# Last stage of a graph network: the own messages gathered plainly into buffers of their own and added by VectorE

## The chip, the cores and the metric

One core of one Trainium2 chip runs the whole network in a single launch. The metric is the device time of that launch in microseconds. The engines are TensorE (PE in the rows, with its weight loads as PEld), VectorE (DVE), ScalarE (ACT), GpSimd (POOL) and SyncE (SP, which here only issues DMAs).

## The reference, cut to what matters

The network has four layers over 10000 nodes (padded to 10240) of 512 features: graph attention, a mixture of 16 experts, a graph convolution of two steps, and a mixture of 8 experts. The change lies in the last kernel stage, which ends the convolution and does the second mixture:

```python
self_term = diag[:, None] * (x @ W0)
msgs = edge_vals[:, None] * (x @ W1)[edge_src]
neigh = segment_sum(msgs, edge_dst, num_segments=n)
h = relu(self_term + neigh + b)          # second step of the convolution
y = (h + x) * 0.5
...
logits = xf @ router_w                    # xf: layer-normed rows
for e in range(E):
    h = relu(xf @ w1[e] + b1[e]) @ w2[e] + b2[e]
    out = out + w[:, e] * layernorm(xf + h, gamma[e], beta[e])
```

`self_term + b` is in HBM as `own` when the stage begins, and the summed messages of a node that has any are a row of `message2`; a node without messages points to a row of zeros.

## The kernel before

`dense1_phase` works on 20 groups of 512 nodes (`NG`, `GR`), each group as 4 tiles `t` of 128 nodes (`T`, `P`) with 512 features in the free dimension. It is a pipeline written out by hand: every engine has a `body(i, c_)`, which `bodies` runs for c_ = 0, then in a loop of 4 passes with 4 bodies each, then four more times, 21 in all. In body g an engine works for several groups at once: the end of group g-1, the experts of group g, the transposes of g+1, the sums of g+2 and the loads of g+3. Within an engine the order is the order of the code; between engines there are counting semaphores.

The way of a tile of group g before the experts:

- SyncE loads the own rows into `own[n]`, n = g % 2 (`load_own`, L2299), once `summed` says that the buffer is free.
- GpSimd copies the row numbers to `at`, waits for `own_in`, and gathers from `message2` with an indirect DMA that adds to what lies in `own[n]` (`gather`, L2342); it raises `msg_in`.
- ScalarE waits for `msg_in` and does 0.5 * relu in place with a sum over features (`half`, L2379). That comes last in its body. The next body begins with two `norm` (L2408) for the transposes.
- ScalarE scales the loaded `y` (`scale_y`), VectorE adds (`sum_`, L2540), ScalarE squares, VectorE and GpSimd (`power`) make mean and scale, ScalarE does `norm`, TensorE transposes the tile (`turn`, L2744), ScalarE copies the high part (`high`, L2413) and VectorE makes the rest (`low`, L2564).

VectorE's body begins with `coefficients` of group g-1 (L2628 on), then `mean_of` (L2533, needs the four `half` of g+2), `routing` (L2596 on), the first `low`, and ends with `finish` of g-1, whose last instruction is L2661 for tile 3 and waits for TensorE's last product of the body. TensorE's body begins with `up(g, 0)`, twelve matmuls; then `turn(g+1, 0)`, `up(g, 1)`, `turn_coef`, `turn(g+1, 1)`, the cross products, `turn` 2 and 3, logits, squares (L2762), and the products of g-1. `turn` t needs the `norm` of its tile and the `low` of the tile before.

Of the kernel before, what the change touches and what calls it, by code (L numbers as in the profile page):

```python
# [24 lines left out]
ALU = mybir.AluOpType  # L25
# [3 lines left out]
P = 128  # L29
D = 512  # L30
# [3 lines left out]
T = 4  # L34
# [6 lines left out]
EP = ET * P  # L41
# [6 lines left out]
XS = 4  # L48
# [2166 lines left out]
def dense1_phase(nc, a, k, ex, out):  # L2215
# [5 lines left out]
    with ExitStack() as stack:  # L2221
        c = Core(nc, stack, "d1")
        x3 = [c.sb(f"x3{n}", [P, T, D]) for n in range(XS)]
        xf, res = c.sb("xf", [P, T, D]), c.sb("res", [P, T, D])
        own = [c.sb(f"own{n}", [P, T, D]) for n in range(2)]
        squared = c.sb("squared", [P, T, D], BF16)
        at = c.sb("at", [P, T], I32)
        gain = c.sb("gain", [P, T])
        xh, xl = ([c.sb(f"{n}{i}", [P, KC, GR], F32R) for i in range(2)] for n in ("xh", "xl"))
# [27 lines left out]
        y_in = [[c.sem(f"y_in{u}{t}") for t in range(T)] for u in range(XS)]  # L2257
        own_in = [[c.sem(f"own_in{n}{t}") for t in range(T)] for n in range(2)]
        msg_in, out_done = ([c.sem(f"{n}{t}") for t in range(T)] for n in ("msg_in", "out_done"))
        at_made, relu_done, gains, affine, summed = (c.sem(n) for n in ("at_made", "relu_done", "gains", "affine", "summed"))  # L2260
        means, squares_made, stats, pow_done, shifted, normed = (
            c.sem(n) for n in ("means", "squares_made", "stats", "pow_done", "shifted", "normed"))
# [22 lines left out]
        def in_range(i, c_, ahead):  # L2285

            return not isinstance(i, int) or 0 <= c_ + ahead < NG
# [41 lines left out]
        @block.gpsimd  # L2329
        def _(pool):  # L2330
            def gather(i, c_):
                g, n = i * XS + c_, c_ % 2
                if later(i, c_):
                    for t in range(T):
                        pool.wait_ge(msg_in[t], 16 * g)
                hold(pool)
                pool.tensor_copy(at[:], k.slot["d"][:, ds(T * g, T)]).then_inc(at_made, 1)
                pool.wait_ge(at_made, g + 1)
                for t in range(T):
                    pool.wait_ge(own_in[n][t], i * 32 + 16 * (c_ // 2 + 1))  # L2340
                    hold(pool)
                    pool.indirect_dma_start(own[n][:, t, :], None, k.message2[:, :],  # L2342
                                            bass.IndirectOffsetOnAxis(ap=at[:, t:t + 1], axis=0),
                                            bounds_check=EP + P - 1, compute_op=ALU.add).then_inc(msg_in[t], 16)

            def power(g):
                pool.wait_ge(stats, g + 1)
                pool.tensor_tensor(rs[:], ve[:], k.half_neg[:, 0:T], ALU.pow).then_inc(pow_done, 1)

            def power2(g):  # L2350
                pool.wait_ge(vars_, NVAR * g + NVAR)
                pool.tensor_tensor(rs2[:].rearrange("p t n -> p (t n)"), var2[:].rearrange("p t n -> p (t n)"),
                                   k.half_neg[:, 0:T * 2], ALU.pow).then_inc(pow2_done, 1)

            def body(i, c_):
                g = i * XS + c_
                if in_range(i, c_, 3):
                    gather(i, c_ + 3)
                if in_range(i, c_, 2):
                    power(g + 2)  # L2360
                if in_range(i, c_, 0):
                    power2(g)

            gather(0, 0)
            gather(0, 1)
            power(0)
            gather(0, 2)
            power(1)
            bodies(pool, body)

        @block.scalar
        def _(act_):
            def half(i, c_, t):

                g, n = i * XS + c_, c_ % 2
                act_.wait_ge(msg_in[t], 16 * g + 16)
                if t == 0 and later(i, c_):
                    act_.wait_ge(means, g)
                act_.activation(own[n][:, t, :], own[n][:, t, :], ACT.Relu, scale=0.5,  # L2379
                                accum_out=own_sum[:, t:t + 1]).then_inc(relu_done, 1)  # L2380
# [127 lines left out]
        def _(v):  # L2508
# [7 lines left out]

            def wide(t_):
                return t_.unsqueeze(2).broadcast_to(S3)

            def gains_of(i, c_):  # L2520
                g = i * XS + c_
                if later(i, c_):
                    v.wait_ge(affine, 4 * g)
                hold(v)
                v.tensor_scalar(gain[:], k.dev[:, ds(T * g, T)], 0.5, None, ALU.add).then_inc(gains, 1)

            def mean_of(i, c_):
                g = i * XS + c_
                v.wait_ge(relu_done, 4 * g + 4)
                if later(i, c_):  # L2530
                    v.wait_ge(squares_made, 4 * g)
                    v.wait_ge(shifted, NSHIFT * g)
                v.tensor_scalar(less_mean[:], own_sum[:], -1.0 / D, None, ALU.mult).then_inc(means, 1)  # L2533
# [15 lines left out]
            def shifts(i, c_):  # L2549

                g, u = i * XS + c_, c_ % XS
                s = Steps(v, shifted, NSHIFT * g)
                v.wait_ge(pow_done, g + 1)
                s(v.tensor_copy(pair[u][:, :, 0], rs[:]))
                s(v.tensor_tensor(pair[u][:, :, 1], less_mean[:], rs[:], ALU.mult))
                s.link(v.tensor_tensor(spread_sq[:], square_sum[:], rs[:], ALU.mult))
                s.link(v.scalar_tensor_tensor(msq[:], spread_sq[:], 1.0 / D, rs[:], ALU.mult, ALU.mult))
                s(v.tensor_tensor(base[c_ % 2][:, :, EXPERTS1:LOGITS], wide(msq[:]),
                                  ex.square[:].unsqueeze(1).broadcast_to(S3), ALU.add))
                assert s.n == NSHIFT  # L2560
# [91 lines left out]
            def finish(i, c_, t):  # L2652

                g, u = i * XS + c_, c_ % XS
                v.wait_ge(x_done, 4 * g + t + 1)
                if later(i, c_):
                    v.wait_ge(out_done[t], 16 * g)
                v.tensor_tensor(res[:, t, :], x3[u][:, t, :], pox[t][:], ALU.mult).then_inc(mul_done, 1)
                v.wait_ge(one_done, 4 * g + t + 1)
                v.wait_ge(mul_done, 8 * g + 2 * t + 1 + 16)  # L2660
                v.tensor_tensor(res[:, t, :], res[:, t, :], po1[t][:], ALU.add).then_inc(mul_done, 1)  # L2661

            def body(i, c_):
                g, n, n1 = i * XS + c_, c_ % 2, (c_ + 1) % 2
                front, mid, main, behind = (in_range(i, c_, ahead) for ahead in (2, 1, 0, -1))
                if behind:
                    coefficients(g - 1, n1, (c_ - 1) % XS)
                if front:
                    mean_of(i, c_ + 2)
                if main:  # L2670
                    routing(g, n)
                if mid:
                    low(g + 1, n1, 0)
                if main:
                    hidden_low(g, n, 0)
                if front:
                    sum_(i, c_ + 2, 0)
                if main:
                    hidden_low(g, n, 1)
                if mid:  # L2680
                    low(g + 1, n1, 1)
                if front:
                    sum_(i, c_ + 2, 1)
                if behind:
                    scale(g - 1, n1, 0)
                if mid:
                    low(g + 1, n1, 2)
                if main:
                    quadratic(g, n, 0)
                if behind:  # L2690
                    weighted_low(g - 1, 0)
                if front:
                    sum_(i, c_ + 2, 2)
                    sum_(i, c_ + 2, 3)
                if mid:
                    low(g + 1, n1, 3)
                if behind:
                    scale(g - 1, n1, 1)
                if main:
                    quadratic(g, n, 1)  # L2700
                if behind:
                    weighted_low(g - 1, 1)
                if front:
                    variance_of(i, c_ + 2)
                    if in_range(i, c_, 3):
                        gains_of(i, c_ + 3)
                    shifts(i, c_ + 2)
                if behind:
                    finish(i, c_ - 1, 0)
                if main:  # L2710
                    variance(g, n)
                if mid:
                    logits_of(g + 1, n1)
                if behind:
                    for t in range(1, T):
                        finish(i, c_ - 1, t)

            gains_of(0, 0)
            mean_of(0, 0)
            for t in range(T):  # L2720
# [1 line left out]
            variance_of(0, 0)  # L2722
            gains_of(0, 1)
            shifts(0, 0)
            mean_of(0, 1)
            for t in range(T):
                sum_(0, 1, t)
# [2 lines left out]
            gains_of(0, 2)  # L2730
            shifts(0, 1)
            logits_of(0, 0)
            bodies(v, body)

        @block.tensor
# [229 lines left out]
```

## Time and profile before

| | |
|---|---|
| median of 3 runs | 2803.28 us (2800.49 to 2804.03) |
| the profiled execution | 2806.13 us, its span 2803.8 us |
| mean granted TensorE clock | 0.932 of full speed |
| TensorE, VectorE, ScalarE, GpSimd busy over the span | 87%, 63%, 41%, 24% |
| last stage | from about 2166 us to the end |

The page cuts the span into 40 slices of 70 us; the last nine are the last stage. The busy share is an average over an engine's order of work: an engine that idles may still be the one that is waited for at one point of each body, and an engine that waits long may be waiting where nobody needs it. So the shares are read together with the chain that ended last and the timeline of a single turn from body to body.

### The profile page before, as it was taken

To read this page: it belongs to the slowest core of one execution; us is meant where nothing else is said; L and a number is where in the kernel's file an instruction comes from. 1 tells how busy PE (TensorE), PEld (TensorE's weight loads), DVE (VectorE), ACT (ScalarE), POOL (GpSimd) and SP (SyncE) were. 2 spreads that over 40 slices of the span, in tenths; PEclk is the share of its full clock that TensorE was granted. 3 is DMA by queue.
4 is the path that set the end of the run, shared out by engine and by line. 5 is a ranking of instruction groups with operands and counts; after the bars stand their busy time and mean duration, and the time that the engine had idled before them with its cause. 6 is when DMAs were issued, how large, how long until landed. Compare 5 with 4: busy or idle time off the path is not lost. (4 is left out here: it accounts for less than half of the span.)

```text
span 2803.8 us, 37672 instructions
## 1 busy us (share of the span) xinstructions
PE 2428.5 (87%) x10876; PEld 1881.2 (67%) x10876; DVE 1772.8 (63%) x4089; ACT 1139.5 (41%) x2071; POOL 670.9 (24%) x675
## 2 busy tenths in 40 slices
PE   5698829399999999999957999999966499999998
PEld 4465617277777777777745888888854377777776
DVE  7454287577777777777544555555556377777775
ACT  6453301344354453444343222222232565665651
POOL 5444300311121111211021221221221333333320
PEclk8799959699999999999978999999987699999999
DMA  4112001411211212211043334334352655656531
GB/s 134 46 31 52 11 4 70 156 61 50 87 69 67 90 56 80 89 50 57 31 157 105 130 128 132 129 126 133 118 160 90 171 132 132 163 129 165 135 105 46
DMA packets 156248, 271.68 MB, mean 97 GB/s; under 512 B 35618, under 2 KB 36258, under 8 KB 155878
## 3 DMA queue, kind: packets, MB, share of 16 engines
q1 hardware_dynamic: 122854, 202.74, 21.5%
q0 software_dynamic: 33280, 67.71, 10.8%
q8 instruction: 36, 0.59, 0.1%
q14 instruction: 78, 0.64, 0.1%
HBM read 186.35 MB, written 100.41 MB: 102 GB/s over the span
## 5 line engine op out<-in xcount | busy, mean ns | idle before, releaser
L1053 POOL TENSOR_TENSOR d_rs<-d_ve,net_half_neg 128x4 f32<-128x4 f32 x60 | 61.2, 1019 | 563.0 <-DVE d_ve L1109 471.0
L1931 ACT ACTIVATE conv_h<-conv_h 128x512 f32<-128x512 f32 x80 | 50.6, 632 | 310.4 <-DVE conv_h L1893 310.4
L2342 POOL DMA_INDIRECT d_own<-message,d_at x80 | 130.6, 1633 | 162.6 <-DMA d_own<-own 142.6
L1863 DVE TENSOR_TENSOR conv_yl<-conv_pty,conv_yh 128x512 fp32r<-128x512 f32 x80 | 55.4, 692 | 180.1 <-ACT conv_yh L1927 168.0
L1374 ACT ACTIVATE d_act_out<-d_pa 128x512 f32<-128x512 f32 x80 | 46.7, 584 | 243.7 <-PE d_pa L67 243.7
L65 PE MATMUL d_po<-d_w_hi,d_hh 128*128 128x512 f32 x320 | 132.2, 413 | 14.0 <-DVE d_x L1200 14.0
L65 PE MATMUL conv_p<-conv_w_hi,conv_yh 128*128 128x512 f32 x320 | 133.8, 418 | 0.6 <-DVE conv_yl L1863 0.6
L65 PE MATMUL d_pa<-d_xh,d_w_hi 128*128 128x512 f32 x320 | 132.4, 414 | 0.5 <-DVE d_w_lo L1126 0.5
L1066 POOL DMA_INDIRECT d_val<-values,d_at x80 | 87.8, 1098 | 185.7 <-DVE d_x L1187 165.6
L65 PE MATMUL d_pc<-d_xh,d_w_hi 128*128 128x512 f32 x320 | 131.6, 411 | 0.0
L66 PE MATMUL d_pa<-d_xl,d_w_hi 128*128 128x512 f32 x320 | 128.9, 403 | 0.0
L67 PE MATMUL d_pa<-d_xh,d_w_lo 128*128 128x512 f32 x320 | 128.7, 402 | 0.0
L65 PE MATMUL conv_p<-conv_w_hi,conv_hh 128*128 128x512 f32 x320 | 126.2, 395 | 1.4 <-DVE conv_hl L1863 1.4
L66 PE MATMUL conv_p<-conv_w_lo,conv_yh 128*128 128x512 f32 x320 | 127.3, 398 | 0.0
L67 PE MATMUL conv_p<-conv_w_hi,conv_yl 128*128 128x512 f32 x320 | 127.1, 397 | 0.0
L67 PE MATMUL d_pc<-d_xh,d_w_lo 128*128 128x512 f32 x320 | 126.9, 397 | 0.0
L66 PE MATMUL d_pc<-d_xl,d_w_hi 128*128 128x512 f32 x320 | 126.6, 396 | 0.0
L67 PE MATMUL conv_p<-conv_w_hi,conv_hl 128*128 128x512 f32 x320 | 126.6, 396 | 0.0
L66 PE MATMUL conv_p<-conv_w_lo,conv_hh 128*128 128x512 f32 x320 | 126.5, 395 | 0.0
L67 PE MATMUL d_po<-d_w_hi,d_hl 128*128 128x512 f32 x320 | 126.3, 395 | 0.0
L66 PE MATMUL d_po<-d_w_lo,d_hh 128*128 128x512 f32 x320 | 126.1, 394 | 0.0
L1486 PE MATMUL d_ptr<-net_ident,d_xf 128*128 128x128 f32 x320 | 52.8, 290 | 61.8 <-ACT d_xf L1363 51.2
(513 smaller groups left out, 7213.3 us busy)
## 6 DMA issues: line engine op xcount, KB each, us to landing
d_x<-in_x SPq DMA_DIRECT2D x20, 1024.0 KB, 7.2
y<-d_y SPq DMA_DIRECT2D x80, 256.0 KB, 2.0
conv_yin<-y SPq DMA_DIRECT2D x80, 256.0 KB, 2.7
h<-conv_h SPq DMA_DIRECT2D x80, 256.0 KB, 2.0
own<-conv_own SPq DMA_DIRECT2D x80, 256.0 KB, 2.0
d_own<-own SPq DMA_DIRECT2D x80, 256.0 KB, 4.1
d_x<-y SPq DMA_DIRECT2D x80, 256.0 KB, 2.8
out<-d_res SPq DMA_DIRECT2D x80, 256.0 KB, 2.5
```

The source lines that it names most:

```text
L65: te.matmul(out, lhs[0], rhs[0], start=first, stop=False, skip_group_check=True)
L66: te.matmul(out, lhs[0], rhs[1], start=False, stop=False, skip_group_check=True)
L67: return te.matmul(out, lhs[1], rhs[0], start=False, stop=last, skip_group_check=True)
L1053: pool.tensor_tensor(rs[n][:], ve[n][:], k.half_neg[:, 0:T], ALU.pow).then_inc(pow_done[n], 1)
L1066: pool.indirect_dma_start(val[:, t, :], None, k.values[:, :], bass.IndirectOffsetOnAxis(ap=at[:, t:t + 1], axis=0), bounds_check=EP + P - ...
L1374: act_.activation(act_out[:, cc % 2, :], pa[cc % 2][:], ACT.Tanh, scale=0.5).then_inc(tanh_done, 1)
L1486: last = pe.transpose(ptr[:, kc * P:kc * P + P], xf[:, t, kc * P:kc * P + P], k.ident[:])
L1863: v.tensor_tensor(lo[:, t % 2, :], bank[t % 2][:], hi[:, t % 2, :].bitcast(F32), ALU.subtract)\
L1931: act_.activation(h[:, t, :], h[:, t, :], ACT.Relu).then_inc(h_made, 1)
L2342: pool.indirect_dma_start(own[n][:, t, :], None, k.message2[:, :], bass.IndirectOffsetOnAxis(ap=at[:, t:t + 1], axis=0), bounds_check=EP + ...
```

## The change

The gather loses its accumulation and goes to two new buffers `got`, so it no longer waits for the own rows; it waits until the buffer's earlier group was added. VectorE gets `add`, four instructions for each group, which wait for both the own rows and the messages and raise `added`; `half` waits for `added` in place of `msg_in`. In the steady part the adds of group g+3 are the last thing in VectorE's body g. Those of groups 0 to 2 stand in the code ahead of the bodies. The two buffers take 2 x 128 x 2048 float32 of SBUF.

```diff
+        got = [c.sb(f"got{n}", [P, T, D]) for n in range(2)]
...
+        added = c.sem("added")
...
                 for t in range(T):
-                    pool.wait_ge(own_in[n][t], i * 32 + 16 * (c_ // 2 + 1))
+                    if not isinstance(i, int) or c_ >= 2:
+                        pool.wait_ge(added, 4 * (g - 2) + t + 1)
                     hold(pool)
-                    pool.indirect_dma_start(own[n][:, t, :], None, k.message2[:, :],
+                    pool.indirect_dma_start(got[n][:, t, :], None, k.message2[:, :],
                                             bass.IndirectOffsetOnAxis(ap=at[:, t:t + 1], axis=0),
-                                            bounds_check=EP + P - 1, compute_op=ALU.add).then_inc(msg_in[t], 16)
+                                            bounds_check=EP + P - 1, oob_is_err=False).then_inc(msg_in[t], 16)
...
             def half(i, c_, t):
...
-                act_.wait_ge(msg_in[t], 16 * g + 16)
+                act_.wait_ge(added, 4 * g + t + 1)
...
+            def add(i, c_, t):
+
+                g, n = i * XS + c_, c_ % 2
+                v.wait_ge(own_in[n][t], i * 32 + 16 * (c_ // 2 + 1))
+                v.wait_ge(msg_in[t], 16 * g + 16)
+                v.tensor_tensor(own[n][:, t, :], own[n][:, t, :], got[n][:, t, :], ALU.add).then_inc(added, 1)
...
                 if behind:
                     for t in range(1, T):
                         finish(i, c_ - 1, t)
-
+                if in_range(i, c_, 3):
+                    for t in range(T):
+                        add(i, c_ + 3, t)
+
+            for t in range(T):
+                add(0, 0, t)
             gains_of(0, 0)
             mean_of(0, 0)
...
             shifts(0, 0)
+            for t in range(T):
+                add(0, 1, t)
             mean_of(0, 1)
...
             logits_of(0, 0)
+            for t in range(T):
+                add(0, 2, t)
             bodies(v, body)
```

## Rows read from the trace of the kernel before

**Rows 1.** Windows: us, then busy us (instructions) of each engine, TensorE clock, DMA share, GB/s.

```profile
2400.00:2500.00 100.00, 96.85 (x437) 74.37 (x436) 73.38 (x188) 59.69 (x130) 32.17 (x25) 0.98 0.59 138
```

**Rows 2.** Groups by line, GpSimd: busy us, mean ns, idle before and its releasers.

```profile
L2342 POOL DMA_INDIRECT d_own<-message,d_at x80 | 130.6, 1633 | 162.6 <-DMA d_own<-own 142.6 <-issue 16.5 <-POOL d_at L2337 3.5
L1066 POOL DMA_INDIRECT d_val<-values,d_at x80 | 87.8, 1098 | 185.7 <-DVE d_x L1187 165.6 <-issue 18.3 <-POOL d_at L1084 0.9
```

**Rows 3.** Chain that ended last, one body: start us, us, what.

```profile
2403.86 1.72 PE d_psm L2762 x4
...
2423.62 0.70 DVE d_xl L2564
...
2424.46 0.63 PE d_ptr L2744 x4
...
2431.95 1.72 PE d_psm L2762 x4
```

**Rows 4.** Timeline of VectorE at a turn: start us, us, instruction, idle before.

```profile
2414.35 0.69 DVE L2661 TENSOR_TENSOR d_res<-d_res,d_px 128x512 f32<-128x512 f32 x1 [0.57 <-PE d_px L67]
2414.96 0.16 DVE L2628 COPY d_terms<-net_mean 128x4 f32 x1
...
2419.82 0.69 DVE L2564 TENSOR_TENSOR d_xl<-d_ptr,d_xh 128x512 fp32r<-128x512 f32 x1
```

**Rows 5.** Timeline of ScalarE at the same turn.

```profile
2407.95 0.62 ACT L2379 ACTIVATE d_own<-d_own 128x512 f32<-128x512 f32 x1
...
2408.56 1.52 ACT L2408 ACTIVATE d_xf<-d_x,d_pair 128x512 f32<-128x512 f32 x2
2417.55 0.23 ACT L2434 ACTIVATE d_prob<-d_prob 128x32 f32<-128x32 f32 x1 [7.47 <-DVE d_prob L2597]
```

**Rows 6.** Timeline of TensorE at the same turn.

```profile
2414.06 0.40 PE L65 MATMUL d_pu<-d_xh,ex_w_hi 128*128 128x512 f32 x1
...
2416.88 0.60 PE L2744 MATMUL d_ptr<-net_ident,d_xf 128*128 128x128 f32 x4
...
2420.66 0.63 PE L2744 MATMUL d_ptr<-net_ident,d_xf 128*128 128x128 f32 x4
```

**Rows 7.** DMA issues of the page: KB each, median us to landing.

```profile
d_own<-message,d_at POOLq DMA_INDIRECT x80, 5.7
```

**Rows 8.** Timeline of VectorE, ScalarE and TensorE at a jump back in the loop.

```profile
2470.17 0.69 DVE L2661 TENSOR_TENSOR d_res<-d_res,d_px 128x512 f32<-128x512 f32 x1 [0.57 <-PE d_px L67]
2474.24 0.17 DVE L2628 COPY d_terms<-net_mean 128x4 f32 x1 [3.38 <-issue]
...
2464.38 1.51 ACT L2408 ACTIVATE d_xf<-d_x,d_pair 128x512 f32<-128x512 f32 x2
...
2479.75 1.09 PE L2744 MATMUL d_ptr<-net_ident,d_xf 128*128 128x128 f32 x4 [2.96 <-ACT d_xf L2408]
...
2481.07 0.63 PE L66 MATMUL d_pq<-d_xl,ex_w2t_hi 128*128 128x512 f32 x1
...
2482.77 0.42 PE L67 MATMUL d_pq<-d_xh,ex_w2t_lo 128*128 128x512 f32 x1
```

**Rows 9.** Timeline of VectorE on the way into the loop.

```profile
2243.80 0.22 DVE L2631 TENSOR_TENSOR d_spare<-d_chosen,d_rs 128x64 f32<-128x64 f32 x1 [1.04 <-POOL d_rs L2352]
```

**Rows 10.** Chain that ended last, start of the stage.

```profile
2175.42 8.52 DMA d_own<-message,d_at
...
2190.92 7.76 DMA d_own<-message,d_at
```

**Rows 11.** Timeline of GpSimd, first gathers of groups 0 and 1.

```profile
2169.76 1.63 POOL L2342 DMA_INDIRECT d_own<-message,d_at  x1 [3.32 <-DMA d_own<-own]
...
2185.21 1.71 POOL L2342 DMA_INDIRECT d_own<-message,d_at  x1 [0.85 <-POOL d_at L2337]
```

**Rows 12.** Timeline of TensorE in earlier stages, behind two idle stretches.

```profile
480.16 0.47 PE L65 MATMUL agg_po<-agg_w_hi,agg_ah 128*128 128x512 f32 x1 [2.37 <-DVE agg_al L824]
...
1493.33 0.80 PE L65 MATMUL msg_po<-conv_w_hi,msg_sh 128*128 128x512 f32 x1 [2.54 <-DVE msg_sl L1704]
```

## The prediction

> **What bounds the kernel now.** I read the page's forty slices first: from about 2240 us to the end TensorE's digits are 9. The table of windows confirms it for the middle of the last stage: TensorE busy 96.85 of 100 us, VectorE 73.38, ScalarE 59.69, GpSimd 32.17 [rows 1]. So TensorE sets the pace, but with little room.
>
> The groups by line and their waits come next, because they hold the lure of this case: the longest wait that the change can remove is GpSimd's for the own rows, 142.6 us [rows 2]. Before believing it one has to ask who waits for the result. The chain that ended last answers: in the steady part it never goes through a gather. It goes through TensorE, and at the turns from one body to the next through VectorE and ScalarE back to TensorE [rows 3]. So the 142.6 us are cover, not cost; only the start of the stage has gathers in its chain.
>
> The change puts its work at the turn between bodies, so I read the timeline there engine by engine. VectorE starts the last add of `finish` (L2661) at 2414.35 and goes straight on with `coefficients` at 2414.96 and, behind `routing`, with the first `low` at 2419.82, done at 2420.51 [rows 4]. ScalarE has by then long done its four `half` (the last starts at 2407.95) and the next body's first two `norm` (2408.56, 1.52 us for both, done 2410.08); then it idles 7.47 us until VectorE's `prob` lets the exponential go [rows 5]. TensorE starts `up` at 2414.06, takes `turn` 0 at 2416.88 and `turn` 1 at 2420.66 [rows 6]. Two things are to be seen. `turn` 1 starts 0.15 us after `low` ended, so the path finish, coefficients, routing, low on VectorE is already as long as TensorE's own. And `turn` 0 has its `norm` 6.8 us early, because ScalarE's `half` is done in an idle stretch.
>
> **The change, part by part.**
>
> *The gather* becomes the plain form. 80 accumulating ones take 1633 ns of GpSimd each, 80 plain ones of the same size in an earlier stage 1098 [rows 2]: 0.5 us less each. In the steady part that is worth nothing, nor is the wait that goes: a body lasts 28.09 us (L2762 at 2403.86 and 2431.95 [rows 3]), the four gathers some 4 x 1.4 us of issue and 5.7 us to landing [rows 7], so they are in about 17 us before `add` asks for them.
>
> *The own wait* stands on VectorE now, in front of everything queued there. The own load is issued early in a body, takes about as long, and is needed at the body's end. I cost it at nothing; what hides it is some 20 us of the other work, and without them VectorE and behind it TensorE would stand for each late microsecond.
>
> *The adds.* Four more VectorE instructions of 128x512 float32 for each group. The nearest row is L2661, which starts 0.61 us before the instruction behind it and lasts 0.69 [rows 4]. VectorE idles 26 us in 100, room enough in the mean for 2.4 us in 28. But the adds are written last in the body, behind a `finish` that waits for TensorE's last product, and VectorE takes them in order, so none of the idle time ahead of it is used. `coefficients` and all behind it start 4 x 0.605 = 2.42 us later.
>
> *The wait of `half`* moves from the landing to `added`, and on ScalarE the next `norm` is queued behind `half`. The adds run from 2414.96, the fourth is done at 2417.47, the last `half` takes 0.61, so `norm` starts at about 2418.15 and is done at 2418.95. TensorE wants it at 2416.88 [rows 6] and stands for 2.1 us. This is not added to the 2.42: after `turn` 0 and twelve matmuls TensorE comes to `turn` 1 at about 2422.75, while `low` now ends at 2422.93. Both paths agree; the turn costs 2.4 us in all. Slack that could hide it would have to show, and `turn` 2 too follows its `low` (2423.62 + 0.70) by 0.14 us [rows 3].
>
> *How many turns.* Adds stand in bodies 0 to 16. Turns within the loop: 3 in each of 4 passes, 12; and the one out of the loop: 13 x 2.42 = 31.5 us.
>
> *The three jumps back.* Here VectorE stands 3.38 us between the last `finish` (2470.17) and `coefficients` (2474.24), ScalarE goes on without a gap (2464.38), and TensorE idles 2.96 us before `turn` 1 [rows 8]. The adds can run inside VectorE's pause if its sequencer hands them over and goes on to the jump. Bounds: 0 each (all covered) and 2.4 (none). ScalarE doesn't set it: by the steps above its `norm` is done at about 2474.8, 2 us after `turn` 0 is wanted, and TensorE had 2.96 us to stand anyway. I take 1.5 each, 4.5 us, as each add brings two waits that the sequencer has to pass first. The Trainium skill (Perfetto Trace Analysis, on the DVE / Act engine instruction) says that the sequencer pushes an instruction into a wait queue and is ready for the next one before its semaphores are met; by that these adds are covered and the sum is 4.5 us lower. ScalarE's `norm`, which follows `half` across the jump without a gap, agrees [rows 8].
>
> *Into the loop.* Body 0 has no `finish`, and `coefficients` stands 1.04 us for GpSimd [rows 9]. The adds fill that: 2.4 - 1.0 = 1.4 us, bounds 0 and 2.4.
>
> *The start.* Here gathers are the chain: 8.52 us and 7.76 us to landing [rows 10]. The first stands 3.32 us for the own rows; of these 0.85 stay, as for group 1's first [rows 11], so 2.5 go. Four shorter issues bring 0.5 us each from the second on: the fourth of group 0 goes at about 2171.3 in place of 2175.42. Landing I leave at its 8 us, since the loads of `y` run beside it. Group 1 follows when group 0 has landed, again with shorter issues, so its last lands at 2192.2 or so in place of 2198.68. One add of 0.69 us comes between landing and `half`: 6 us gained. Bounds: 3 (ScalarE's `scale_y` is held by the `y` loads) and 8 (landing is quicker too). The adds of group 2 I cost at nothing: TensorE is at its lower clock then, `turn` 0 is wanted 5 us after the first matmul, and if that cover failed they would cost 2.4.
>
> *TensorE's clock.* Behind the idle 2.96 us, matmuls run at the lower level, 1.2 GHz: five starts from 2481.07 to 2482.77, 0.43 us apart [rows 8], where twelve took 2.82 us, 0.235 each [rows 6]. With the transposes before them that is some 1.2 us lost. A stretch of 2.37 us elsewhere did not bring it (the next matmul lasted 0.47), one of 2.54 us did (0.80) [rows 12]. Mine is 2.1 us, below both, though with small pauses near it. I give it to a quarter of the 13 turns: 13 x 0.25 x 1.2 = 4 us; bounds 0 and 15.6.
>
> **Sum.** 31.5 + 4.5 + 1.4 - 6 + 4 = 35.4 us. The profiled execution took 2806.13 us with a span of 2803.8 us; every term lies in the span, so it would be 2841.5. The median of the runs is 2.85 us below that execution, so 2838.5 us, 1.3% slower.
>
> **Rivals.**
> 1. *Faster.* The start gains 6 us and the adds vanish in VectorE's idle time. It decides if each turn has over 2.4 us of slack: 2803.3 - 6 = 2797 us. For it: VectorE is busy for three quarters only. Against: the 0.15 us from `low` to `turn` 1. 3%.
> 2. *The clock falls at every turn*: 15.6 in place of 4: 2850 us. For it: 2.54 us were enough once. Against: 2.37 were not. 20%.
> 3. *Half is absorbed*, by an order on ScalarE or TensorE that gives back half of each turn: 2803.3 + 16 + 1.4 - 6 + 2 = 2817 us. 9%.
> 4. *No change*: 0.5 us left over at each turn, which the start gives back: 2803 us. 3%.
> 5. *The adds wait for data*, and VectorE with them, beyond some 17 us of cover: 2 us at each of 16 bodies would make 2870 us. Nothing in the rows speaks for it. 3%.
> The forecast has 62%.
>
> **How the numbers follow.** The forecast's own range is 2826 (jumps and clock free, start 8) to 2848. The range of 8 in 10 takes in rival 2 and reaches towards 3: 2822 to 2854. A difference below 0.2% (5.6 us) can't be told from none here. Slower: 62 + 20 + 9 + 3 = 94%, less 1 for the edge of rival 3: 93%. Same 4%, faster 3%.
>
> **What would show it.** Right: gathers of 1.1 us without a wait for own rows; adds of 0.69 us directly behind the last L2661 of a body; 2.1 us of idle TensorE ahead of `turn` 0, released by `norm`; some 30.5 us between bodies where it was 28.09; the stage's first `norm` 6 us earlier; at the jumps VectorE's adds inside its pause. Wrong: bodies still near 28 us, so that the adds found room; matmuls of 0.63 us behind every turn (rival 2); an add whose releaser is a DMA (rival 5).

## The result: 1.1% slower, and the profile after

The changed kernel takes 2835.44 us (median of 4 runs, 2833.11 to 2836.96); the kernel before, measured beside it, 2803.66 us (4 runs, 2800.49 to 2813.16). The ratio is 1.0107, with a 95% interval of 1.0082 to 1.0132. The profiled execution took 2836.30 us with a span of 2834.5 us, 30.7 us longer than the span before.

The window that answers to [rows 1]. TensorE lost 3.7 us of busy time in 100, VectorE gained 4.6, GpSimd lost 10.9:

```profile
2400.00:2500.00 100.00, 93.12 (x414) 71.57 (x414) 78.00 (x187) 57.04 (x121) 21.24 (x21) 0.97 0.39 126
```

The groups by line, for GpSimd, and for VectorE's adds (L2528). The gathers, now L2345, take 1087 ns and never wait for own rows, where they stood 142.6 us [rows 2]. The adds last 689 ns each, and their whole wait for a DMA is 8.9 us, all of it at the start of the stage:

```profile
L2345 POOL DMA_INDIRECT d_got<-message,d_at x80 | 87.0, 1087 | 36.7 <-issue 18.3 <-POOL d_at L2339 16.6 <-DVE d_own L2528 1.8
L2528 DVE TENSOR_TENSOR d_own<-d_own,d_got 128x512 f32<-128x512 f32 x80 | 50.5, 689 | 8.9 <-DMA d_got<-message,d_at 8.9
```

The waits of the whole execution name the new one: ScalarE's `half` (L2382) for the adds, once in every group.

```profile
ACT d_own L2382 <- DVE d_own L2528: 195.1, 20, 35.8
```

Most of those 195.1 us are idle time that ScalarE has in any case; what counts is when the wait ends. The timeline of VectorE at an ordinary turn answers to [rows 4]. From the start of the last L2671 to `coefficients` (L2638) it was 0.61 us and is 3.07:

```profile
2449.24 0.69 DVE L2671 TENSOR_TENSOR d_res<-d_res,d_px 128x512 f32<-128x512 f32 x1 [0.57 <-PE d_px L67]
2449.84 2.54 DVE L2528 TENSOR_TENSOR d_own<-d_own,d_got 128x512 f32<-128x512 f32 x4
2452.31 0.16 DVE L2638 COPY d_terms<-net_mean 128x4 f32 x1
```

ScalarE at the same turn, to be held against [rows 5]. There `half` ran in an idle stretch 6.4 us ahead of VectorE's last `finish`; here it begins behind the first add, and `norm` stands behind the fourth:

```profile
2450.56 0.63 ACT L2382 ACTIVATE d_own<-d_own 128x512 f32<-128x512 f32 x1 [9.47 <-DVE d_own L2528]
...
2452.45 0.61 ACT L2382 ACTIVATE d_own<-d_own 128x512 f32<-128x512 f32 x1
...
2453.06 1.50 ACT L2411 ACTIVATE d_xf<-d_x,d_pair 128x512 f32<-128x512 f32 x2
```

The chain that ended last now runs through these pieces (start us, us, what), where [rows 3] had none of them:

```profile
2449.84 0.70 DVE d_own L2528
...
2451.10 0.76 ACT d_own L2382 x3
...
2453.15 1.41 ACT d_xf L2411 x2
```

TensorE at two ordinary turns. `turn` 0 (L2763) stands 1.99 us at both. Behind the first, `up` goes on at 0.235 us from start to start; behind the second at 0.43 until 2330.77:

```profile
2296.94 0.66 PE L2763 MATMUL d_ptr<-net_ident,d_xf 128*128 128x128 f32 x4 [1.99 <-ACT d_xf L2411]
...
2297.67 0.40 PE L66 MATMUL d_pu<-d_xl,ex_w_hi 128*128 128x512 f32 x1
2297.90 0.40 PE L67 MATMUL d_pu<-d_xh,ex_w_lo 128*128 128x512 f32 x1
...
2327.13 0.85 PE L2763 MATMUL d_ptr<-net_ident,d_xf 128*128 128x128 f32 x4 [1.99 <-ACT d_xf L2411]
...
2328.21 0.63 PE L66 MATMUL d_pu<-d_xl,ex_w_hi 128*128 128x512 f32 x1
2328.63 0.63 PE L67 MATMUL d_pu<-d_xh,ex_w_lo 128*128 128x512 f32 x1
```

The windows of the same two stretches show the granted clock: 1.00 (2.4 GHz) and 0.55, that is, mostly the lower level of 1.2 GHz:

```profile
2296.90:2300.00 3.10, 3.06 (x15) 2.57 (x16) 2.83 (x13) 3.10 (x7) 0.00 (x0) 1.00 1.00 341
2327.10:2330.30 3.20, 3.17 (x10) 2.64 (x11) 2.92 (x13) 3.20 (x7) 0.00 (x0) 0.55 1.00 388
```

A jump back, VectorE, to be held against the first two rows of [rows 8]. The four adds follow `finish` at once and lie inside the pause; 2.30 us of pause are left behind them:

```profile
2353.83 0.69 DVE L2671 TENSOR_TENSOR d_res<-d_res,d_px 128x512 f32<-128x512 f32 x1 [0.57 <-PE d_px L67]
2354.43 2.49 DVE L2528 TENSOR_TENSOR d_own<-d_own,d_got 128x512 f32<-128x512 f32 x4
2359.22 0.17 DVE L2638 COPY d_terms<-net_mean 128x4 f32 x1 [2.30 <-issue]
```

The chain at the start of the stage answers to [rows 10]: 6.29 us to landing, then one add, then ScalarE.

```profile
2168.80 6.29 DMA d_got<-message,d_at
...
2175.18 0.69 DVE d_own L2528
```

**A ruler for all runs.** The place of the last stage in the span is no constant. Its first own load is issued at 2166.22 us before and at 2163.75 after, and in the other traces between 2160.0 and 2173.0, with the same code ahead of it; one and the same program gave 2171.6 and 2161.6. So I measure inside the stage: its length from that first load to the end of the span, the start of the first `squares` from it, and the periods between the starts of `squares` of neighbouring groups. "Ordinary" periods cross the 13 turns that don't jump, "jump" periods the three that do.

| kernel | stage, us | first `squares` | ordinary periods | jump periods |
|---|---|---|---|---|
| before | 637.6 | 71.2 | 27.7 to 28.1 | 32.2, 32.4, 32.2 |
| after | 670.8 | 61.6 | 30.1 to 30.2 (7), 31.3 to 31.4 (6) | 33.9, 32.5, 33.0 |
| adds early | 634.6 | 63.1 | 27.7 to 28.0 | 33.6, 34.5, 32.5 |
| `half` behind `norm` | 671.9 | 62.5 | 30.1 to 30.2, 31.4 | 34.5, 34.6, 34.2 |
| no adds, two traces | 634.2; 638.4 | 58.6; 61.6 | 27.7 to 28.1 | 34.6, 34.6, 35.3; 34.8, 35.1, 35.5 |
| adds twice | 727.8 | 69.1 | 33.7 to 34.3 | 34.3, 34.4, 34.3 |
| adds on GpSimd | 671.6 | 69.0 | 27.7 to 29.8 | 38.7, 36.5, 38.8 |
| gather waits for own | 667.1 | 64.4 | 30.1 to 30.2, 31.3 to 31.4 | 31.4, 31.2, 31.8 |
| before, written out | 621.1 | 71.8 | 27.6 | 27.6 |
| after, written out | 661.9 | 62.7 | 30.0 to 30.3 (8), 31.3 (8) | among them |
| two adds late, written out | 632.1 | 62.2 | 28.8 to 28.9 | 29.1 at most |
| adds early, written out | 614.5 | 63.4 | 27.7 to 27.8 | 28.0 at most |
| no adds, written out | 610.6 | 61.2 | 27.6 | 27.6 |

### The profile page after: what moved, and what is told of

Its sections match the earlier page's. It is cut to its first block and busy times, and to the rows that moved or that the text cites. A ratio compares the mean times of both kernels' runs of the same rounds, so it can differ in the third digit from the quotient of the medians.

```text
span 2834.5 us, 37874 instructions
## 1 busy us (share of the span) xinstructions
PE 2437.9 (86%) x10873; PEld 1886.2 (67%) x10876; DVE 1821.4 (64%) x4169; ACT 1141.2 (40%) x2071; POOL 627.1 (22%) x675
## 5 line engine op out<-in xcount | busy, mean ns | idle before, releaser
L1053 POOL TENSOR_TENSOR d_rs<-d_ve,net_half_neg 128x4 f32<-128x4 f32 x60 | 61.2, 1020 | 561.0 <-DVE d_ve L1109 469.0
L2382 ACT ACTIVATE d_own<-d_own 128x512 f32<-128x512 f32 x80 | 49.5, 620 | 195.1 <-DVE d_own L2528 195.1
L2763 PE MATMUL d_ptr<-net_ident,d_xf 128*128 128x128 f32 x320 | 52.8, 290 | 76.6 <-ACT d_xf L2411 66.8
```

The source lines that it names most:

```text
L1053: pool.tensor_tensor(rs[n][:], ve[n][:], k.half_neg[:, 0:T], ALU.pow).then_inc(pow_done[n], 1)
L2763: last = pe.transpose(ptr[:, kc * P:kc * P + P], xf[:, t, kc * P:kc * P + P], k.ident[:])
```

## The experiments

### First four: the place of the adds, their number, and none

**Adds early.** The four adds of group g+3 move from the end of VectorE's body to the place ahead of `shifts`, where it waits for GpSimd's scale.

```diff
                     if in_range(i, c_, 3):
                         gains_of(i, c_ + 3)
+                        for t in range(T):
+                            add(i, c_ + 3, t)
                     shifts(i, c_ + 2)
...
-                if in_range(i, c_, 3):
-                    for t in range(T):
-                        add(i, c_ + 3, t)
```

> The change with the four adds of each group moved on VectorE from the end of the body to the place between gains_of and shifts, where VectorE waits for GpSimd's power; nothing else. If the cost of the change is the adds' place in the order (the prediction's steps on the adds and on half), each turn goes back to 27.7 to 28.1 us, the idle stretch ahead of turn 0 goes, and only the gain at the stage's start is left, which the trace of the change puts at 8 to 10 us: 2793 to 2797 us. If the adds cost their 2.4 us of VectorE wherever they stand (the engine has no room in its order, or two-input adds hold up its neighbours), it stays at 2830 to 2837. In between (2810) if finish and its product wait for the adds by half a microsecond or more for each group.

Measured: 2805.99 us (12 runs) against 2804.11 before, ratio 1.0002, interval 0.9989 to 1.0014. The cost is gone: ordinary periods are 28 us again, with the same 80 adds. The gain of the start (8 us by the first `squares`) did not show in the total. The table says where more than half of it went: the jump periods are 1.4, 2.0 and 0.3 us longer than before, and the 13 ordinary ones together 1 us. The other 3 us are left inside the stage (634.6 against 637.6), less than its place in the span moves from trace to trace. The pause itself is longer, though it holds no adds now:

```profile
2353.38 0.69 DVE L2671 TENSOR_TENSOR d_res<-d_res,d_px 128x512 f32<-128x512 f32 x1 [0.57 <-PE d_px L67]
2358.46 0.17 DVE L2638 COPY d_terms<-net_mean 128x4 f32 x1 [4.39 <-issue]
```

**`half` behind `norm`.** The adds stay last; ScalarE does its four `half` behind the first two `norm` of the next body (those of group 2, ahead of the bodies, move along).

```diff
                 if mid:
                     norm(i, c_ + 1, 0)
                     norm(i, c_ + 1, 1)
+                if front:
+                    for t in range(T):
+                        half(i, c_ + 2, t)
...
-                if in_range(i, c_, 3):
-                    for t in range(T):
-                        half(i, c_ + 3, t)
```

> The change with ScalarE's four half moved behind the first two norm of the next body; the adds stay at the end. This takes away only ScalarE's part of the turn. If both paths are equally long, as the prediction says, the time stays within 3 us of the change's 2835: the idle stretch of 2.0 us ahead of turn 0 is gone, and one of about 2.4 us stands ahead of turn 1, since low is still 2.4 us later. If the wait of half on added is what costs and VectorE's delay is hidden, turns go back to 28 us and the time to about 2796.

Measured: 2840.7 us (4 runs), ratio 1.0136, 1.0114 to 1.0157; the stage is 671.9 us against 670.8 after. The total is 2.7 us above the expected 3 us around 2835; the stage is within it. TensorE's idle stretch moves from `turn` 0, released by `norm`, to `turn` 1, released by `low`, and stays as long:

```profile
2428.09 0.75 PE L2761 MATMUL d_ptr<-net_ident,d_xf 128*128 128x128 f32 x4 [2.05 <-DVE d_xl L2572]
2459.49 0.63 PE L2761 MATMUL d_ptr<-net_ident,d_xf 128*128 128x128 f32 x4 [2.05 <-DVE d_xl L2572]
```

So ScalarE's order is no remedy: VectorE's own path is as late. The two paths are two faces of one delay.

**No adds.** The gathers stay, the messages are never added, and ScalarE waits for both loads directly.

```diff
-                if in_range(i, c_, 3):
-                    for t in range(T):
-                        add(i, c_ + 3, t)
...
-                act_.wait_ge(added, 4 * g + t + 1)
+                act_.wait_ge(own_in[n][t], i * 32 + 16 * (c_ // 2 + 1))
+                act_.wait_ge(msg_in[t], 16 * g + 16)
```

> The change without its adds: the messages are gathered into their buffers but never added to the own rows (this part of the computation is left out), and half waits for both landings. It prices the plain gather and the lost wait for own rows alone. Expected 2792 to 2797 us: 8 to 10 us less than before, all in the stage's start, turns at 27.7 to 28.1 us. If the gain at the start was only the execution's luck, 2803. Against e1 it gives the price of well placed adds: 0 to 2 us by my reading.

Measured: 2800.9 us (10 runs), ratio 0.9992, 0.9981 to 1.0003. Ordinary periods are those of before within 0.1 us, so the adds were the whole cost there. But this time is 4 us over the top of the range, and the jump periods are the longest of these four kernels, 34.6 to 35.3 us, with no adds anywhere. My expectation had taken the pause as a constant; it is not.

**Adds twice.** Each add is preceded by another of the same operands into a spare buffer.

```diff
+                v.tensor_tensor(twice[:, t, :], own[n][:, t, :], got[n][:, t, :], ALU.add).then_inc(doubled, 1)
                 v.tensor_tensor(own[n][:, t, :], own[n][:, t, :], got[n][:, t, :], ALU.add).then_inc(added, 1)
```

> The change with a second VectorE addition of the same shape ahead of each add, its result thrown away: eight instructions at each turn. If each adds 0.605 us at 13 turns and TensorE's idle stretch of now 4.4 us brings the lower clock at all 13 turns in place of the 6 seen, then 13 x 2.42 + 7 x 1.2 = 40 us more, and 2 us each at the three jumps and the way in: 2880 to 2886 us. If the lower clock doesn't depend on the length of the stretch, 8 us less: 2872 to 2878. If VectorE had slack that the first four used up, also the upper value; if it still has some, under 2865.

Measured: 2897.75 us (4 runs), ratio 1.0342, 1.0326 to 1.0359: over the range by 12 us. TensorE stands 4.3 to 4.6 us at every turn, which is the 2.4 us more that was expected, and the lower clock follows at every one of them, as the upper of its ranges had it. What the expectation left out is the start of the stage: with the doubled adds the first `squares` comes 7.5 us later than after (69.1 against 61.6). Two of the turns, with matmuls of 0.63 us behind them:

```profile
2447.67 1.12 PE L2767 MATMUL d_ptr<-net_ident,d_xf 128*128 128x128 f32 x4 [4.40 <-ACT d_xf L2412]
...
2449.01 0.63 PE L66 MATMUL d_pu<-d_xl,ex_w_hi 128*128 128x512 f32 x1
...
2481.90 0.66 PE L2767 MATMUL d_ptr<-net_ident,d_xf 128*128 128x128 f32 x4 [4.40 <-ACT d_xf L2412]
...
2483.30 0.63 PE L65 MATMUL d_pu<-d_xh,ex_w_hi 128*128 128x512 f32 x1
```

At the jumps the eight adds (4.84 us) fill the pause but for 0.71, 0.01 and 0.24 us, and the jump periods are no longer than the others: the pause and the adds overlap, they don't add up.

### Second four: without VectorE's jump, and the adds on another engine

The pause had to be taken out to see the rest. VectorE's program of the stage is written out body by body; the other engines keep their loop.

```diff
-            bodies(v, body)
+            for c_ in range(NG + 1):
+                body(0, c_)
```

**The kernel before, written out.**

> The kernel before with VectorE's program of the last stage written out body by body. If the jump's pause is VectorE's alone, its periods of 32.2, 32.4 and 32.2 us fall to 27.8 and 3 x 4.5 = 13.5 us go: 2790 (2787 to 2794). If the accumulating gathers gave the same time as plain ones with hidden adds, this and the run with early adds written out differ by no more than 2 us; if the earlier start of the stage (8 us to the first norm) is a gain that is kept, this one is 5 to 9 us the slower of the two.

**The changed kernel, written out.**

> The kernel after (adds last in VectorE's program of a body) with VectorE's program written out body by body. If the adds were covered at the jumps by the pause, the jump periods now become ordinary ones of 30.15 to 31.4 us: 3 periods of 33.9, 32.5 and 33.0 give 3 x 2.4 = 7 us back, 2828 (2824 to 2833), and the cost of the change grows to 16 turns x 2.42 = 39 us against the kernel before written out likewise. If the adds were paid at the jumps as well, the gain is the 13 us that the pause costs: 2822 or less.

**Adds early, written out.**

> The adds placed between the products and the shifts, as in the run with the early adds, and VectorE's program of the last stage written out body by body, so that VectorE never jumps back in it. If the three long periods of the run with the early adds (33.6, 34.5 and 32.5 us, against 27.9 for the others) come from VectorE's pause at its jump and from nothing else, they fall to 27.9 and 3 x 5.6 = 17 us go: 2789 (2786 to 2793). If something else at the fourth body makes them long (the rotation of the buffers, the jumps of the other engines), they stay and the time is 2806 (2803 to 2809). The rival to both: a longer program without jumps is fetched no faster, pauses appear at other places, and the gain is half or less, 2797 to 2803.

Measured, against 2806.14 us for the kernel before: 2786.53 us, ratio 0.9932 (0.9915 to 0.9948) for before written out; 2835.2 us, 1.0097 (1.0077 to 1.0118) for after written out; 2783.08 us, 0.9915 (0.9897 to 0.9932) for adds early written out, by median the fastest complete kernel here and faster than both of the case. The window of [rows 1] for before written out:

```profile
2400.00:2500.00 100.00, 100.00 (x460) 77.69 (x460) 76.82 (x200) 60.59 (x132) 30.63 (x25) 1.00 0.60 150
```

for adds early written out:

```profile
2400.00:2500.00 100.00, 100.00 (x466) 78.07 (x465) 85.32 (x215) 61.63 (x128) 28.09 (x27) 1.00 0.50 168
```

and for after written out:

```profile
2400.00:2500.00 100.00, 94.02 (x423) 72.58 (x422) 77.72 (x187) 59.65 (x125) 22.21 (x21) 0.97 0.39 128
```

In the first two TensorE is busy without a gap at full clock in that window, and all 16 periods behind the first are 27.6 to 28.0 us: the long periods at the fourth bodies were VectorE's jump and nothing else, since the other engines still jump there. The 13 ordinary periods of before fell too, from 27.84 to 27.60 us in the mean, 3 us of the 16.5 that the stage gained.

The traces also show what stands beside VectorE's pause, which its rows mark `<-issue`: idle time in which it waits for no semaphore that the profile shows. In each of the nine traced kernels with VectorE's loop, at each of the three jumps, one transfer of 8 KB on an instruction queue falls between the last `finish` and `coefficients`, 1.5 to 4.2 us behind the start of that `finish`, and `coefficients` starts 1.2 to 1.8 us after the transfer has ended. In the kernel before, at the jump of [rows 8], it runs from 2472.19 to 2472.50 us; the DMA queues of the window 2472.1 to 2472.6 (packets, MB, share):

```profile
q14 instruction: 1, 0.01, 3.9%
```

In the five traced kernels with VectorE's program written out no transfer of that kind falls between `finish` and `coefficients` at these three turns. The queue does not name its engine; that the transfer is VectorE's is inferred from this comparison.

In the third, the change costs its full price at all 16 turns: eight periods of 30.08 us in the mean, 2.48 over the 27.60 of before written out, and eight of 31.3, another 1.22 for the lower clock. 16 x 2.48 + 8 x 1.22 = 49.4 us; the first period adds 1.3, the start gives 9.0 back; the stage is 40.8 us longer.

Two of the three came out 0.5 us (before) and 3 us (adds early) under their ranges. The early start of the stage, 8.4 us by the first `squares`, leaves adds early 6.6 us ahead of before written out inside the stage and 3.4 us by the medians, where the two intervals overlap: a gain of the plain gather at the start is likely and, by total time, not shown. The expectation for after written out (2828, up to 2833) missed by median, at 2835.2. Its stage is 8.9 us shorter than that of after, but began 8.2 us later in the profiled execution, so by total time the two can't be told apart in four runs each.

Two neighbouring turns of it, the first at full clock behind the stretch, the second at the lower (matmuls of 0.63 us). What TensorE did ahead of them is the same program, and I found no difference that decides:

```profile
2458.12 0.66 PE L2764 MATMUL d_ptr<-net_ident,d_xf 128*128 128x128 f32 x4 [1.92 <-ACT d_xf L2411]
...
2458.85 0.40 PE L66 MATMUL d_pu<-d_xl,ex_w_hi 128*128 128x512 f32 x1
...
2488.20 0.66 PE L2764 MATMUL d_ptr<-net_ident,d_xf 128*128 128x128 f32 x4 [1.95 <-ACT d_xf L2411]
...
2489.02 0.63 PE L66 MATMUL d_pu<-d_xl,ex_w_hi 128*128 128x512 f32 x1
```

**Adds on GpSimd.** Each four plain gathers are followed by their four adds on GpSimd; VectorE has none.

```diff
                 if in_range(i, c_, 3):
                     gather(i, c_ + 3)
+                    add(i, c_ + 3)
...
+                    pool.tensor_tensor(own[n][:, t, :], own[n][:, t, :], got[n][:, t, :], ALU.add).then_inc(added, 1)
```

> The adds done by GpSimd, behind the plain gathers of the next body and ahead of its powers; VectorE does none. If VectorE's 2.42 us a turn are the whole cost, it is gone and the time is that of the run without adds, 2801 (2797 to 2808), provided that four adds of GpSimd (bounded by 0.7 us each, VectorE's, and 2.5 us each) fit into what GpSimd has idle in a body. If GpSimd's adds hold up VectorE, by a shared port or because its powers come late by more than the slack of 17 us, periods rise by the 3 to 10 us of four adds and the time is 2835 or more.

Measured: 2838.14 us (4 runs), ratio 1.0113, 1.0095 to 1.013. It is the second theory, with half of the extra time at the three jumps. A GpSimd add takes 1.30 us in the median; no run had stood behind the 2.5 us of the upper bound. GpSimd's adds, from the timeline of GpSimd:

```profile
2366.92 5.30 POOL L2354 TENSOR_TENSOR d_own<-d_own,d_got 128x512 f32<-128x512 f32 x4 [5.34 <-DMA d_own<-own]
```

and VectorE in that stretch:

```profile
2366.94 1.52 DVE L2612 TENSOR_TENSOR d_wins<-d_logit 128x256 f32<-128x256 f32 x1
2368.49 1.37 DVE L2614 TENSOR_TENSOR d_wins<-d_wins,ex_earlier 128x256 f32<-128x256 f32 x1
2369.90 0.42 DVE L2615 TENSOR_REDUCE d_rank<-d_wins 128x32 f32<-128x256 f32 x1
```

The two `d_wins` instructions take 0.42 us each elsewhere; the reduction, with one input, keeps its 0.42. The Trainium skill (GPSIMD Engine Reference, the row on SBUF interfaces) says that GpSimd shares its SBUF interfaces with VectorE and contends with those of its instructions that have two inputs in SBUF; the trace agrees. At the jumps the adds fall into `routing`, which TensorE waits for (6.60 us ahead of `turn` 1, released by `low`), and the periods reach 38.8 us. They fall there because they come late: in 16 of the 20 groups GpSimd stands for the own rows, 78.2 us in all.

### Last four: the size of each piece

**Two adds late.** VectorE's program is written out; two of the four adds stand last, two early.

```diff
                         gains_of(i, c_ + 3)
+                        for t in (0, 1):
+                            add(i, c_ + 3, t)
...
-                    for t in range(T):
+                    for t in (2, 3):
                         add(i, c_ + 3, t)
```

> As the run with late adds written out body by body, but only two of a body's four adds stand last; the other two stand where the early ones did. If what costs is VectorE's time ahead of turn 0, two adds there cost about half: 8 adds made TensorE idle 4.4 us and 4 adds 1.9 us, so 2 adds some 0.7 us and 1.2 us of period, 16 x 1.2 = 19 us over the run with early adds written out: 2802 (2799 to 2806), with no lower clock behind the gap. If the clock falls behind gaps of 0.7 us as often as it did behind those of 1.9 us, add 8 x 1.25 = 10 us: 2812. If the cost is that of a wait for data or of the order and not of the work, it is all there or all gone: 2835 or 2784.

Measured: 2799.18 us (10 runs), ratio 0.9972, 0.9961 to 0.9984, in the first theory's range. TensorE's idle stretch is 0.65 to 0.72 us, and none is followed by the lower clock:

```profile
2437.35 0.66 PE L2766 MATMUL d_ptr<-net_ident,d_xf 128*128 128x128 f32 x4 [0.70 <-ACT d_xf L2411]
...
2438.07 0.40 PE L66 MATMUL d_pu<-d_xl,ex_w_hi 128*128 128x512 f32 x1
2438.31 0.39 PE L67 MATMUL d_pu<-d_xh,ex_w_lo 128*128 128x512 f32 x1
```

**No adds, written out.** As the run without adds, with the edit of the second four: the messages are gathered and never added.

> The changed kernel without the adds (the own messages are gathered but never added), and VectorE's program written out body by body. If the run without adds missed its 2792 to 2797 because VectorE's pause at the jump was longer in that program (its jump periods were 34.6, 34.6 and 35.3 us), the periods are now 27.6 to 27.7 and the time is 3 us under the run with early adds written out: 2780 (2777 to 2784). If the plain gathers or their waits cost something of their own, it is 2787 or more, over the kernel before written out.

Measured: 2775.4 us (4 runs), ratio 0.9888, 0.9861 to 0.9916, 1.6 us under the range. The periods are 27.6 us. The looped run's jump periods had exceeded those of before by 7.7 us in all; without that its 2800.9 us would be 2793, inside its range. So the pause was the reason why the run without adds had missed. Early adds cost 0.16 us in a period of 27.76, and 2.2 us at the start (first `squares` 63.4 against 61.2), 3.9 us over the stage; by medians the difference is 7.7 us, and the two intervals just overlap.

**Gather waits for own.** The changed kernel, with the old wait put back on GpSimd.

```diff
                     if not isinstance(i, int) or c_ >= 2:
                         pool.wait_ge(added, 4 * (g - 2) + t + 1)
+                    pool.wait_ge(own_in[n][t], i * 32 + 16 * (c_ // 2 + 1))
```

> The changed kernel, but GpSimd still waits for the loads of the own rows ahead of each plain gather, as the accumulating gather had to. In the middle of the stage that wait ends far ahead and costs nothing. At the start it gives back the part of the gain that comes from not waiting: the gathers start some 2.5 us later, norm 0 comes 2.5 us later, and the time is 2838 (2836 to 2840). If the start's gain of 8 us comes from that wait alone, all 8 go: 2843. If it comes from the plain gather's quicker landing alone, nothing goes: 2835.

Measured: 2828.36 us (4 runs), ratio 1.0086, 1.0056 to 1.0116: the total misses all three ranges, and does not stand apart from after. Inside the stage the piece comes out as the first theory has it: TensorE's first `turn` starts 28.49 us into the stage, 25.98 in after, so the wait is worth 2.5 us. It is hidden in the total by a stage that began 3.8 us earlier in the profiled execution, and by jump periods of 31.4, 31.2 and 31.8 us, 4.9 us less than in after, although VectorE's program is the same there, instruction for instruction:

```profile
2353.38 2.49 DVE L2529 TENSOR_TENSOR d_own<-d_own,d_got 128x512 f32<-128x512 f32 x4
2357.00 0.17 DVE L2639 COPY d_terms<-net_mean 128x4 f32 x1 [1.13 <-issue]
```

**No adds, a second trace.**

> The run without adds once more, the program unchanged, for a second trace of it. If the length of VectorE's pause at the jump back belongs to the program (where its code lies), the three long periods are again 34.6, 34.6 and 35.3 us, within 0.3. If it belongs to the execution, they differ from those by 1 us or more and may be as short as the 32.2 of the kernel before. The start of the last stage, 2166.2, 2163.8, 2160.0, 2169.6 and 2172.2 us in five programs with the same code ahead of it, is read beside it in the same way.

Measured: one run of 2801.68 us. The jump periods are 34.8, 35.1 and 35.5 us, after 34.6, 34.6 and 35.3; one differs by 0.5 us, two by 0.2. VectorE's pause itself is 4.97, 4.93 and 5.35 us, after 5.42, 4.54 and 4.96: 0.4 us either way. That is nearer to "belongs to the program" than to "belongs to the execution", since programs with the adds early, absent or done by the gather lie between 32.2 and 35.5; but it is one pair of traces. The start of the stage did change, by 10.0 us in the same program.

## Why the prediction was right, point by point

The forecast was 2838.5 us, the result 2835.4. Two slips of arithmetic stand in it: 2841.5 less 2.85 is 2838.7, and with the jumps and the clock free and a start of 8 the sum gives 2828, not 2826 (2827 with the way into the loop free as well). Neither matters to the outcome. Its sum was 35.4 us against a span 30.7 us longer; 2.5 us of that difference is the earlier stages' drift (the stage began at 2163.75 and not 2166.22), the rest is in the terms.

- **What to believe of the waits.** GpSimd's 142.6 us for own rows went and gave nothing but the start's share of it. Right, and the chain of [rows 3] was what said so.
- **The adds at ordinary turns**, 13 x 2.42 = 31.5. The seven periods without a lower clock average 30.16 us, the 13 of before 27.84: 2.3 us each, 30.2 in all. Right. (The expected 30.5 us between bodies came from the one period of 28.09 read; most are 27.73.) The path was the predicted one: `norm` starts 3.22 us behind the first add (3.19 by the working), TensorE stands 1.99 us (2.1). That it is VectorE's queue and not the data is shown by the same adds early (gone), two late (1.1 us over all early), eight (4.4 us of idle), and none.
- **"Both paths agree."** Shown by `half` behind `norm`: the idle stretch changed its releaser and its place, not its length.
- **The clock**, 4 us for a quarter of the turns. Six of 13 periods were 1.2 us longer: 7.2 us. Under-sized, inside its bounds. A stretch of 1.99 us, below the 2.37 that had brought no lower clock in [rows 12], did bring it, so those two stretches had given no threshold; that the term lies inside its bounds is owed to their width.
- **The jumps**, 4.5 us. Measured 1.7, 0.1 and 0.8 = 2.6. The mechanism that the bound of 0 stood for is what the trace shows: adds start 0.6 us behind `finish`, inside the pause. By the Trainium skill (Perfetto Trace Analysis, on the DVE / Act engine instruction) the sequencer hands an instruction over and goes on; the traces agree, most clearly the one of eight adds, where 0.71, 0.01 and 0.24 us of pause are left behind them. The reason given for taking 1.5 each, that the sequencer must first pass two waits for each add, is borne out by no run. The 2.6 us can't be split further, since the pause has another length in every program.
- **Into the loop**, 1.4 us: 2.1 measured, with the lower clock behind it. In after written out, where the clock did not fall at that turn, it is 1.3.
- **The start**, 6 us: the first `norm` came 8.1 us earlier into the stage, the upper bound. 2.5 of them are the own wait, as worked out; 1.7 are the shorter issues of group 0, and 2.2 its quicker landing (6.29 us in place of 8.52), which I had left as it was. The last 1.7 come behind that: the chain no longer goes through group 1's landing, but through VectorE's and ScalarE's work on group 0 to the adds of group 1. By the first `squares` it was 9.6 us; TensorE reached full clock 41 us into the stage, where it had been 57.
- **Rivals.** Faster, no change, half absorbed and waiting for data did not happen: the ordinary periods and the 8.9 us of waits on a DMA exclude them for this kernel. A lower clock at every turn happened only with eight adds.

Sum of the measured terms: 37.4 (adds and clock) + 2.6 + 2.1 - 9.6 + 0.7 at the end = 33.2 us inside the stage (637.6 to 670.8), less 2.5 of drift. That the total agrees to 3 us is partly luck: the terms are off by up to 3.6 us each, in both directions, and the place of the stage alone moves by more than 3 us between traces. What stands without luck is the largest term, the adds at ordinary turns, and its path.

What stays open: why one stretch of 1.9 to 2.0 us is followed by the lower clock and the next is not, and what sets the length of VectorE's pause. That code in a loop must be fetched again is what the traces point to: writing the program out removed the pause, and in each pause stands a transfer on an instruction queue, behind whose end VectorE goes on. The Trainium skill (Runtime: NRT & Kernel Launch, Instruction fetch mechanics) says that a taken branch out of the fetched part stalls its engine; the traces agree. The transfer lasts 0.3 to 0.9 us; what varies most is how late it starts, and why is not shown. Where the code lies, which might explain the spread between programs, was not tried.

## What to carry to other kernels

Ask of an added instruction not how idle its engine is but what stands behind it in that engine's queue. Behind the last thing that waits for the bottleneck engine, four small adds cost 2.5 us per body, and 3.1 with what the clock adds; in front of a wait of their own engine the same four cost 0.16. As it stood, the change removed a wait behind which, in the steady part, nobody waited, and paid for it at the turn. And compare small changes with the loop's jump taken out: here its pause moved by 1 to 3 us from one program to the next and hid gains as large as the change's own.

## What the runs showed of the hardware that was not expected

- VectorE's jump back costs 4.3 to 7.6 us of period in the kernels whose adds are early, absent or done by the gather (32.2 to 35.5 us, against 27.8 to 28.0 in the mean of the others), three times in the stage. The jumps of the other engines cost nothing that shows: they are still there in before written out, where all 16 periods are 27.6 us. In each pause of VectorE, 27 in nine traces, stands one 8-KB transfer on an instruction queue, and VectorE goes on 1.2 to 1.8 us behind its end. Its length differs between programs whose VectorE instructions are the same: 33.9, 32.5, 33.0 us after, and 31.4, 31.2, 31.8 with one more wait on GpSimd.
- Idle stretches of TensorE of 1.9 to 2.0 us were followed by the lower clock in 6 of 13 turns (after) and 8 of 16 (written out), those of 0.65 to 0.72 us in none, those of 4.3 to 4.6 us in all.
- GpSimd's add of two 128x512 float32 inputs takes about 1.3 us (5.30 for four), VectorE's 0.69; VectorE's own instructions with two inputs in SBUF went from 0.42 to 1.4 and 1.5 us beside it.
- The plain gather takes 1087 ns of GpSimd where the accumulating one takes 1633, and lands in 6.3 us at the start of the stage instead of 8.5.
